# Attention, output projection and FFN in one kernel: a unit's last two transposes in the outputs' bank, and a set's fourteen output products shared out 3, 4, 3, 4

## What is computed

```python
x = hidden_states                       # (4, 512, 1024)
xn = layernorm(x)
q, k, v = split(xn @ w_qkv)             # 32 query heads, 8 key/value heads, D = 128
s = q @ k.T * D**-0.5 - slope[h] * sqrt(i - j), masked to j <= i
attn = softmax(s) @ v                   # each group of 4 query heads shares k and v
ffn = xn @ W.T + b + top1-of-4-ranks LoRA of xn
out = x + attn.reshape(4, 512, 4096) @ w_o + ffn
```

## Time and profile before

| | us |
|---|---|
| median of 3 runs | 2472.68 (2472.03 to 2477.65) |
| the profiled execution, whole | 2475.28 |
| its span, first to last instruction | 2473.4 |
| TensorE busy | 2377.9 (96%) |
| VectorE busy | 1547.1 (63%) |
| ScalarE busy | 1373.4 (56%) |
| GpSimd busy | 784.2 (32%) |

### The profile page before, as it was taken

One profiled execution on the slowest core, in us unless ns is written; L12 is line 12 of the kernel. 1 busy time (PEld: TensorE's weight loads), 2 busy tenths in 40 slices (PEclk: granted clock), 3 DMA queues, 4 the chain that ended last, 5 costly groups with the idle time before them and its releaser, 6 DMA issues.

```text
span 2473.4 us, 34303 instructions
## 1 busy us (share of the span) xinstructions
PE 2377.9 (96%) x11616; PEld 1991.7 (81%) x11616; DVE 1547.1 (63%) x2969; ACT 1373.4 (56%) x3051; POOL 784.2 (32%) x1029
## 2 busy tenths in 40 slices
PE   5999999998799999999899999999999999999999
PEld 4787888887678788888778888788888888888887
DVE  5657355655655645555676666767667666676665
ACT  4532133334533223333477777777777777777774
POOL 3211000000330100000244645446455464554644
PEclk9999999999899999999999999999999999999999
DMA  4536445546254635445655565655655556666553
GB/s 151 182 129 209 146 146 184 191 170 236 71 175 157 207 120 204 153 170 196 235 185 182 188 230 203 208 194 188 226 201 210 198 188 218 201 211 206 187 175 141
DMA packets 118318, 455.90 MB, mean 184 GB/s; under 512 B 11945, under 2 KB 12089, under 8 KB 109184
## 3 DMA queue, kind: packets, MB, share of 16 engines
q1 hardware_dynamic: 86176, 334.37, 39.2%
q0 software_dynamic: 31968, 119.33, 13.9%
HBM read 276.96 MB, written 176.69 MB: 183 GB/s over the span
## 4 chain that ended last, share of the span: by engine, by line
PE 85%; DVE 5%; ACT 4%; issue 3%; DMA 3%; POOL 1%; SPq 0%; ACTq 0%; DVEq 0%; POOLq 0%
PE ps L677 26%; PE ps L678 26%; PE ps L679 26%; PE ps L877 5%; DMA lora_lo<-lora_s 1%; DMA qk_s<-res_b 1%; ACT probs L1085 1%; ACT res_hi L945 1%; DVE stats L1197 1%; DVE wo L1183 1%; ACT rows L974 1%; PE ps L857 1%; ACT probs L1107 1%; DVE w_lo L1183 0%; DMA qk_s<-res_hi 0%
## 5 line engine op out<-in xcount | busy, mean ns | idle before, releaser
L945 ACT ACTIVATE w_hi<-raw 128x1024 fp32r<-128x1024 f32 x196 | 207.0, 1059 | 558.9 <-PE ps L679 439.5
L1467 DVE TENSOR_TENSOR acc<-ps,acc 128x512 f32<-128x512 f32 x448 | 297.2, 686 | 287.3 <-issue 260.8
L1183 DVE TENSOR_TENSOR w_lo<-raw,w_hi 128x1024 fp32r<-128x1024 f32 x196 | 239.1, 1224 | 357.8 <-ACT w_hi L945 357.6
L677 PE MATMUL ps<-x_hi,w_hi 128*128 128x512 f32 x1120 | 436.5, 390 | 0.0
L678 PE MATMUL ps<-x_lo,w_hi 128*128 128x512 f32 x1120 | 436.0, 389 | 0.0
L679 PE MATMUL ps<-x_hi,w_lo 128*128 128x512 f32 x1120 | 435.9, 389 | 0.0
L1085 ACT ACTIVATE probs<-probs,neg_max 128x512 f32<-128x512 f32 (+3 forms) x512 | 283.9, 566 | 168.8 <-DVE neg_max L1432 168.8
L677 PE MATMUL ps<-wo,op_hi 128*128 128x512 f32 x896 | 363.5, 406 | 2.0 <-POOL op_lo L635 0.7
L678 PE MATMUL ps<-wo,op_hi 128*128 128x512 f32 x896 | 352.1, 393 | 0.0
L679 PE MATMUL ps<-wo,op_lo 128*128 128x512 f32 x896 | 351.5, 392 | 0.0
L679 PEld LDWEIGHTS ps<-x_hi,w_lo 128*128 128x128 f32 x1120 | 210.4, 188 | 43.9
(11 more groups left out here) (166 smaller groups left out, 4637.1 us busy)
## 6 DMA issues: line engine op xcount, KB each, us to landing
raw<-w_all SPq DMA_DIRECT2D x70, 1024.0 KB, 5.4
q<-qk_s SPq DMA_DIRECT2D x128, 512.0 KB, 3.9
acc<-acc_s SPq DMA_DIRECT2D x128, 512.0 KB, 5.1
acc_s<-acc SPq DMA_DIRECT2D x112, 512.0 KB, 7.7
qk_s<-res_hi POOLq DMA_DIRECT2D x40, 1024.0 KB, 4.6
qk_s<-res_a POOLq DMA_DIRECT2D x20, 1024.0 KB, 9.2
qk_s<-res_b POOLq DMA_DIRECT2D x20, 1024.0 KB, 5.2
k<-qk_s SPq DMA_DIRECT2D x32, 512.0 KB, 3.6
```

The source lines that it names most:

```text
L677: pe.matmul(to, st_hi, mv_hi, start=start, stop=False, skip_group_check=True)
L945: nc.scalar.activation(to, source, ACT.Copy).then_inc(signal, 1)
L1183: nc.vector.tensor_tensor(to, source, high.bitcast(F32), ALU.subtract).then_inc(signal, 1)
L1467: nc.vector.tensor_tensor(to, fill[f % 2][:, :], to, ALU.add).then_inc(s_acc, 1)
```

## The change

The third bank of the transposes becomes `ps_o`, where the first half of the attention product goes, and the two waits that `ps_c` had needed are gone. `SHARES` gives the four units of a set 3, 4, 3 and 4 parts in place of 4, 3, 4 and 3.

```diff
-SHARES = (range(0, 4), range(4, 7), range(7, 11), range(11, 14))
+SHARES = (range(0, 3), range(3, 7), range(7, 10), range(10, 14))
...
-        t_banks = [(ps_t0, 0, 512), (ps_t1, 512, 512), (ps_c, 1024, 256)]
+        t_banks = [(ps_t0, 0, 512), (ps_t1, 512, 512), (ps_o, 1024, 256)]
...
                 for c, i in enumerate((3, 2, 0, 1)):
                     if n and i != 1:
                         pe.wait_ge(s_neg_max, QT * (n - 1) + (c + 1 if i else 4))
-                    if n >= 2 and i == 3:
-                        pe.wait_ge(s_pt_lo, 3 * (n - 1))
...
                     if to is ps_t1 and n >= 2:
                         pe.wait_ge(s_at_raw, n // 2)
-                    if to is ps_c and n + 1 < UNITS:
-                        pe.wait_ge(s_neg_max, QT * (n + 1) + 1)
```

## The result

| | before | changed |
|---|---|---|
| median, us | 2473.52 (4 runs) | 2499.32 (4 runs, 2498.35 to 2499.64) |
| span of the profiled execution, us | 2473.4 | 2497.8 |
| TensorE waiting for a maximum, 1262 us to the end of the regular units | 14 times, 17.9 us | none |
| TensorE waiting for an add, the same | none listed | 67 times, 37.0 us |

The ratio is 1.0102, with a 95% interval of 1.0089 to 1.0116: 25.8 us more. The forecast was 2494 us, with a range of 2482 to 2507; against the 2472.68 of the runs shown then that was +21.3 us.

What follows compares the result with a forecast made beforehand. TensorE was taken to bound the kernel, every new wait paid in full: -29.7 us of waits won, +35.6 for 54 regular odd units, +15.4 for seven late units, +21.3 in sum; forecast 2494 us, range 2482 to 2507.

Runs made afterwards that it cites:

- part 1 alone: The kernel before with only the last two transposes moved to the outputs' bank, shares still 4, 3, 4, 3: 2481.33 us against 2474.38, ratio 1.003.

## What to carry to other kernels

A wait that is on the list is not the time that its removal brings: look for the next thing that the same engine would wait for, here the add of two products back, and read from the trace when that ends. When work is moved out from behind a long cover (here 3.5 us of attention product), ask what the moved piece itself waits for; two buffers and an in-order queue mean that the add of its predecessor but one has to be done, and in VectorE's queue that add stood behind the softmax. And often it is the queue's order, not the share of work, that should be changed: one line moved turned +26 us into -15.

## What was not expected of the hardware

- TensorE's granted clock after a standstill. After one of 2.14 us (part 1 alone) it was at half, 1.2 GHz, in five of seven like places; after 1.83 us and, behind a fill, a start 0.26 us late, in one of seven in each of two traces; and after the 67 waits of up to 1.71 us of the changed kernel in none. But after one of 2.38 us (VectorE later in odd units) it was at half in only two of seven places, so the length of the standstill alone does not decide it. Each stretch at half cost 1.2 to 1.5 us. Why some places fall and others do not stays open.
- GpSimd and VectorE together: with both inputs in SBUF, a VectorE split of 128 x 1024 took 1.75 us instead of 1.22 beside GpSimd's sums, and a GpSimd sum of 128 x 256 took 1.71 to 1.73 us instead of 0.74 beside the splits. Both streams lose, because they take turns instruction by instruction.
